# Self-attention's merges of seven head pairs: turned by transposing DMAs in place of TensorE

## The reference, cut to what matters

```
h = layernorm(x)
q, k, v = h @ wq, h @ wk, h @ wv              # 1024 inner columns = 16 heads of 64
attn = softmax(q k^T / 8)                     # per head, 1024 x 1024
x = x + concat_heads(attn @ v) @ wo + bo      # self-attention: the change is in concat_heads(...)
x = x + the same with q from layernorm(x), k and v from the 77 rows of ctx
x = x + (a * gelu(gate)) @ w2 + b2            # a, gate = layernorm(x) @ w1 + b1
```

## Time and profile before

| What | Value |
|---|---|
| median of 3 runs | 2215.81 us |
| profiled execution | 2213.69 us, span 2212.0 us, mean granted clock 0.996 |
| PE busy | 2114.3 us (96%) |
| DVE busy | 1649.8 us (75%) |
| ACT busy | 1473.0 us (67%) |
| POOL busy | 1302.5 us (59%) |
| share of the chain that ended last | PE 80%, DVE 11%, ACT 5% |
| DMA queue of SP | 110.42 MB, 18.4% of 16 engines |
| shift row (1 KB), issue to landing | median 1.9 us |
| `qa`, `ka` moves (128 KB), issue to landing | median 2.3 us |
| weight pieces (512 KB), issue to landing | median 3.5 us |

### The profile page before, as it was taken

The page is one execution under the profiler, slowest core; times in us unless marked ns, Lnnn a source line. Parts: engine busy times, 40 slices in busy tenths (PEclk is TensorE's granted clock), DMA queues, the critical chain, the costliest instruction groups (busy, mean ns, idle before and its releaser), DMA issues.

```text
span 2212.0 us, 59099 instructions
## 1 busy us (share of the span) xinstructions
PE 2114.3 (96%) x25328; PEld 1434.1 (65%) x25328; DVE 1649.8 (75%) x3076; ACT 1473.0 (67%) x1948; POOL 1302.5 (59%) x802
## 2 busy tenths in 40 slices
PE   5999999899999999989999999998999999999899
PEld 2666666675666666767466666675746666667675
DVE  6888887558588888656768888866576888885564
ACT  3888888235488888733548888873355888885442
POOL 5778877223278887722347887862234887774321
PEclk9999999999999999999999999999999999999999
DMA  4322220010232231001032232100103223210000
GB/s 123 82 58 64 76 66 19 11 40 17 72 93 64 64 87 46 28 1 40 25 91 73 64 82 70 45 28 1 40 17 91 83 69 82 54 38 21 11 11 20
DMA packets 77622, 114.20 MB, mean 52 GB/s; under 512 B 26800, under 2 KB 39088, under 8 KB 77360
## 3 DMA queue, kind: packets, MB, share of 16 engines
q1 hardware_dynamic: 77360, 110.42, 18.4%
HBM read 55.72 MB, written 4.19 MB: 27 GB/s over the span
## 4 chain that ended last, share of the span: by engine, by line
PE 80%; DVE 11%; ACT 5%; issue 2%; SPq 1%; POOL 1%; DMA 1%; DVEq 0%; POOLq 0%; ACTq 0%
PE work L884 10%; PE scores L908 9%; PE scores L901 9%; PE scores L798 6%; PE scores L800 6%; PE scores L799 6%; PE work L930 5%; PE work L926 5%; PE work L928 5%; PE work L798 4%; PE work L800 4%; PE work L799 4%; DVE minima L1452 2%; PE work L1080 1%; ACT prob L1270 1%
## 5 line engine op out<-in xcount | busy, mean ns | idle before, releaser
L745 POOL TENSOR_TENSOR prob<-prob 128x1024 f16<-128x1024 f32 x328 | 709.1, 2178 | 296.7 <-ACT prob L1270 280.3
L1452 DVE TENSOR_REDUCE minima<-work 128x1 f32<-128x512 f32 x1024 | 682.0, 684 | 48.4 <-PE work L884 42.4
L1269 ACT ACTIVATE prob<-scores 128x1024 f32<-128x1024 f32 x512 | 526.1, 1028 | 93.3 <-PE scores L908 73.6
L1270 ACT ACTIVATE prob<-scores 128x1024 f16<-128x1024 f32 x512 | 523.2, 1022 | 0.0
L926 PE MATMUL work<-vals,prob 128*128 128x65 f16 x4096 | 428.8, 192 | 2.2 <-POOL prob L745 1.8
L930 PE MATMUL work<-vals,prob 128*128 128x65 f16 x4096 | 429.4, 195 | 0.0
L928 PE MATMUL work<-vals,prob 128*128 128x64 f16 x4096 | 429.2, 193 | 0.0
L926 PEld LDWEIGHTS work<-vals,prob 128*128 128x128 f16 x4096 | 383.0, 99 | 65.8 <-issue 17.6
L884 PE MATMUL work<-ka,qa 128*128 128x512 f16 x1024 | 389.8, 384 | 26.5 <-DVE minima L1452 19.2
L928 PEld LDWEIGHTS work<-vals,prob 128*128 128x128 f16 x4096 | 379.8, 97 | 52.8
L930 PEld LDWEIGHTS work<-vals,prob 128*128 128x128 f16 x4096 | 380.2, 97 | 0.0
(11 more groups left out here) (157 smaller groups left out, 4325.9 us busy)
## 6 DMA issues: line engine op xcount, KB each, us to landing
qa<-staged_q SPq DMA_DIRECT2D x128, 128.0 KB, 2.3
ka<-staged_k SPq DMA_DIRECT2D x128, 128.0 KB, 2.3
raw_even<-in_pairs SPq DMA_DIRECT2D x32, 384.0 KB, 3.3
raw_odd<-in_pairs SPq DMA_DIRECT2D x32, 384.0 KB, 3.2
raw_odd<-in_pieces SPq DMA_DIRECT2D x20, 512.0 KB, 3.5
raw_even<-in_pieces SPq DMA_DIRECT2D x20, 512.0 KB, 3.5
qb<-staged_q SPq DMA_DIRECT2D x64, 128.0 KB, 2.3
kb<-staged_k SPq DMA_DIRECT2D x64, 128.0 KB, 2.3
```

What stands on the lines that cost most here:

```text
L745: pool.tensor_tensor(prob[1][:, slot, :], prob32[:, slot, :], prob[0][:, slot, :], ALU.subtract).then_inc(a.polished, 1)
L1269: act.activation(prob32[:, n % RING, :], source, ACT.Exp)
L1270: act.activation(prob[0][:, n % RING, :], source, ACT.Exp)\
L1452: dve.tensor_reduce(minima[:, t, h:h + 1], out[:, :], AX.X, ALU.max, negate=True)\
```

## The change

Of the eight pairs, seven are no longer merged by PE. Two new kinds of entry, `lay` and `lay_low`, stand in the head 1 unit at steps 2 and 6. In `lay`, ACT copies half of a pair's `o_nat` (128x512, float) to half float in a new SBUF tile `lay`. In `lay_low`, DVE subtracts this from `o_nat`, both from SBUF, into the low part; then SP issues two transposing DMAs of 128x512 half floats, one per part, straight into `oT`. ACT's entry stands before the score of its step; the `lay_low` of DVE and SP stands behind the low part of s-1 and before the value and its gather. The merges of the last pair stay as they were. The tile `xn` now lies in the bytes of `lay`. PE waits for all transposing DMAs before the first output projection.

```diff
-        for at, h in ((4, 0), (6, 1)):
-            placed[at].append(Step("merge", h, 1 - par, 0, -1))
+        for at, h in ((2, 0), (6, 1)):
+            placed[at].append(Step("lay", h, 1 - par, 0, -1))
...
             out += low(TILES - 1, *prv, 2 * pair + head - 1)
+        out += [Step("lay_low", *step[1:]) for step in placed[s] if step.kind == "lay"]
         if s >= LAG:
...
+LAYS_ENDED = ALL["gather"] - 2 * ALL["lay"]
...
-        xn = sb("xn", [P, 4, DIM])
+        lay = sb("lay", [P, 2, 2, BLK], F16)
+        xn = lay[:, :, :, :].rearrange("p s i c -> p (s i) c").bitcast(F32)
...
+                    elif step.kind == "lay_low":                       # SP
+                        s = step.step
+                        sp.wait_ge(a.lay_low, pace.n("lay_low") + 1)
+                        for part in range(2):
+                            sp.dma_start_transpose(oT[part][:, pair, s * BLK:(s + 1) * BLK]
+                                                   .rearrange("p (t q) -> p t q", q=P),
+                                                   lay[:, s, part, :]).then_inc(laid[s], 16)
...
+                for s in range(2):                                     # PE, before the first project
+                    hold(pe, laid[s], (g + 1) * (PAIRS - 1) * 32)
...
+                    elif step.kind == "lay":                           # ACT
+                        act.wait_ge(a.outs_free, pace.n("lay", times=2) + LAYS_ENDED * g + (4 if s == 0 else 3))
+                        before = pace.n("lay") // 2
+                        if before:
+                            act.wait_ge(laid[s], before * 32)
+                        act.activation(lay[:, s, 0, :], o_half(par, s), ACT.Copy).then_inc(a.lay_high, 1)
...
+                    elif step.kind == "lay_low":                       # DVE
+                        dve.wait_ge(a.lay_high, pace.n("lay_low") + 1)
+                        dve.tensor_tensor(lay[:, s, 1, :], o_half(par, s), lay[:, s, 0, :], ALU.subtract)\
+                           .then_inc(a.lay_low, 1)
```

More of the change, by code:

```diff
@@ L456, in build, with o_half @@
         c32 = o_nat[:, :, :, :].rearrange("p a b c -> p (a b c)")[:, 0:BATCH * 2 * CTX_COLS]
+        def o_half(par, s):
+            return o_nat[:, par, s * HALF:(s + 1) * HALF, :].rearrange("p t d -> p (t d)")
         def o_part(s, t):
@@ L491, in build @@
         names = ("peak_full peak_free work_full work_high work_free scores_full exp_done refined polished probs_used "
-                 "outs_free inverse_ready head0_ready head1_ready shift_combined row_ready")
+                 "outs_free inverse_ready head0_ready head1_ready shift_combined row_ready lay_high lay_low")
         a = collections.namedtuple("Sems", names)(*[sem(f"self_{n}") for n in names.split()])
+        laid = [sem(f"laid{h}") for h in range(2)]
         xpeak_full = sem("xpeak_full")
@@ L934, in do @@
                         out = bank()
-                        pe.wait_ge(a.outs_free, pace.n("merge", times=2) + (4 if s == 0 else 3))
+                        pe.wait_ge(a.outs_free, (g + 1) * ALL["gather"] + s)
                         for i in range(HALF):
```

## The result

The changed kernel takes 2302.32 us (median, 2300.76 to 2306.05) against 2215.78 for the kernel before in the same job: a ratio of 1.0393, 95% interval 1.038 to 1.0406. I had forecast 2268 and a range up to 2292: the direction was right, the size was not. The profiled execution has a span of 2299.1 us, 87.1 more than before.

What follows compares the result with a forecast made beforehand. PE, busy for all 42.87 us of a pair, was taken to bound, ACT in last units. Terms 45.4 + 9.6 = 55.0 on 2213.7 gave 2268.7, median 2270.8, trimmed to 2268; own range 2245 to 2285, range given 2198 to 2292.

Steps and rivals of the forecast that it cites:

- head 0 units: The pair's units without the added entries: no loss was booked for them.
- last units: Each round's last unit, where ACT bounds: held subtractions make values late, +2.4 us a round, 9.6 in all.
- head 1 units: Units with the added subtractions: waits less both merges' saving, +2.0 us a pair, +45.4 in all.
- The hold: New DVE subtraction at step 2 starts inside POOL's polish and waits for its end, lasting 1.2 us and more.
- Step 4: In head 1 units, refine falls behind POOL's `wpS` subtraction and is held; PE loses 1.66 us at the maxima.
- Step 6: In head 1 units, the second subtraction is held by a polish, gather and value come late; PE loses 1.2 us.
- The unit without a split: Head 1 unit of round 3's last pair, without `wpS` split: -0.6 us, 0.87 saved less 0.25 of wait.
- the step 2 part: Last unit's first held subtraction: PE loses 2.4 us at the value, ACT's queued work absorbs about 1.2.
- What leaves PE's list is saved at once: PE has no idle time, so removed merges save at most 20.6 us if nobody makes PE wait.
- the rival of 2194: Subtractions find gaps or refine stays ahead of `wpS`; 20.6 us come back, 1 more in last units; chance 0.20.
- The rival of small holds (2211): Refine stays ahead; second subtraction costs 0.25 us a pair, last units 9.6: -5.3 us in sum; chance 0.12.
- The rival of late DMAs: Transposing DMAs over 5.7 us each delay the shift row and next unit's first score: 2268, or 2300 with holds; chance 0.08.

Runs made afterwards that it cites:

- e2: The changed kernel with DVE's subtraction replaced by an operation of the same size reading one SBUF operand (low parts wrong); 2219.4 us.
- e14: The changed kernel with only the last unit's two layings moved: subtractions at steps 0 and 1, DMAs at steps 2 and 3; 2273.7 us.
- e8: The changed kernel without ACT's copies, DVE's subtractions, the transposing DMAs and the waits for them, oT set to zero once; 2211.6 us.
- e3: The changed kernel without ACT's copies and DVE's subtractions; the transposing DMAs still go, from a constant tile; 2205.5 us.

## Why the prediction was right or wrong

Two terms of the sum failed: the head 0 units, where I booked nothing and 16.8 us are lost, and the last units, booked at 9.6 us where 22.6 are lost. The mechanism of the head 1 units held.

**The hold, right.** The subtraction of step 2 was to last 1.2 us; it takes 1.24. e2 shows the cause.

**Step 4, right in sum, not in its parts.** Forecast 1.66 us at the maxima, since refine falls behind `wpS`. The step takes 4.44 us for 2.77: 1.67. But the head 1 unit of pair 6 in round 3 has no `wpS` split, and its step 4 takes 3.32 us for 2.77. So 0.55 us come from refine's lateness alone, where I had nothing, and about 1.1 from the order.

**Step 6, right.** Forecast 1.2; the step behind it takes 4.63 us for 3.44. The unit is 1.98 us longer; forecast +2.0. (A whole pair takes 45.4 us where I had forecast 44.9; the rest is the head 0 unit.) The sum over head 1 units is 46.4, forecast 45.4. The unit without a split, for which I had -0.6, takes 0.87 more (0.55 + 1.19, less the turns' 0.88).

**Head 0 units, wrong.** I carried the walk to the end of the head 1 unit and booked nothing behind it. "1.2 us more" of lateness at step 6 does not end there: refine of step 7 starts 0.09 us behind `wpC` and takes 2.63, and the head 0 unit's first step 3.90 us for 3.34: 11.2 us in 20 units. The six units in which the feed-forward split also holds a refine add 6.6. Less 1.0 of small delays that only the kernel before has there, that is 16.8 in all, the largest single miss of the sum. `wpC` at 723.34 stands in the earlier trace rows, but I did not set the refine of step 7 (721.35 in the same trace) beside it. I did see that the piece of weights would be issued 9 us later. I asked only whether it lands before GpSimd's old time of use, not whose order that changes.

**Last unit, too small.** I took the 2.4 us of step 6 for the round's loss and let ACT's queue swallow the step 2 part. Measured 22.6 us for 9.6. PE stands for 2.36 us at step 2, of which 1.72 reach the last score (14.80 against e14's 13.08), and for 2.33 at step 6. Then it stands for the DMAs, 6.1 us in all, a term that was missing: I had asked how long they may take for the shift row, not who waits for the last two. e2 shows that wait with no held subtraction. The lower clock behind the stalls (10.7 us of PE's busy time by the estimate above) was in no term either. These pieces add up to more than 22.6, so some of them hide each other (round 1 has no wait for the DMAs); how the 22.6 divide among them is open. e14 gives 28.6 us for the move of these layings, which includes the saving of the last unit's missing turns and most of the clock.

**Start of round 0**, 1.3 us, was in no term, and its cause is open; in the other runs of the table it lies between -0.9 and +2.4 (e8, with its setting to zero, apart). The four differences, 1.0 + 16.8 + 13.0 + 1.3, are the 32.1 us between 87.1 and my 55.0.

**"What leaves PE's list is saved at once", wrong,** and with it the rival of 2194. e3 has neither the new hold nor a late DMA and gains 10, not 20.6 us: nothing in pairs 2 to 5, the gain lies in pairs 1 and 6 and at the round's end. The condition that I had put behind it, that nobody makes PE wait, fails by refine 3. The rival of small holds (2211) had the wrong order of refine and `wpS`. The rival of late DMAs fell: 1.25 us of queue and 2.5 to landing.

## What to carry to other kernels

Once a step runs late, follow it until a stretch where it is on time again, past the unit in which it was added, and name every pair of operations whose order hangs on less than the lateness; here an order that stood by 0.12 us was worth about 1.1 of the 1.67 us lost at its step. Where two engines exclude each other, look for the other's idle stretch first (5.7 us here) and put the new operation into it: the same work went from +3.9% to -0.4%. That includes the round's end, where the same move took the stalls, the wait for the DMAs and the clock lost behind them. For data that goes round by DMA, ask of the last one who waits for it, not only whether the queue has room, and look at what else comes later because it stands behind it in the queue.

## What the runs showed of the hardware

```profile
675.45 1.81 POOL L702 TENSOR_SCALAR wpC<-raw_even 128x768 f16<-128x768 f32 x1
```

```profile
751.68 0.83 POOL L702 TENSOR_SCALAR wpS<-raw_odd 128x768 f16<-128x768 f32 x1 [0.70 <-PE work L817]
```
